# An eight-stage transformer kernel: the edges between the attentions in halves, and the last edge before the experts inside the expert steps

## The reference

```python
f0 = causal softmax attention with rotary positions, 16 heads of 8
f1 = feed-forward 128 -> 512 -> 128, SiLU, integer weights with scales, half of it added to its normed input
f2 = attention with its own norm, weights exp(s) * sigmoid(s - mu), normalised
f3 = gated feed-forward 128 -> 384 -> 128
f4 = linear attention (elu + 1), then a GELU feed-forward 128 -> 512 -> 128
f5 = 16 experts of 176, 4 chosen per token in 2 of 4 groups, and a shared expert
f6 = linear attention (elu + 1)
f7 = 8 experts of 512, 2 chosen per token
```

## Time and profile before

| | before |
|---|---|
| median of 3 runs | 1600.1 us (1598.7 to 1605.24) |
| the profiled execution | 1603.26 us |
| its span | 1601.5 us |
| TensorE busy in the span | 1281.2 us (80%) |
| VectorE | 1090.1 us (68%) |
| ScalarE | 1135.8 us (71%) |
| GpSimd | 279.3 us (17%) |
| mean granted TensorE clock | 0.884 |

### The profile page before, as it was taken

How to read it: one execution, slowest core, us unless ns; L and a number is a source line. 1 busy time by engine, 2 the same in 40 slices (tenths; PEclk the granted TensorE clock), 3 DMA queues, 4 the chain that set the end, 5 groups by cost and what they waited for, 6 DMA issues and landing times.

```text
span 1601.5 us, 22150 instructions
## 1 busy us (share of the span) xinstructions
PE 1281.2 (80%) x8028; PEld 650.2 (41%) x8028; DVE 1090.1 (68%) x2035; ACT 1135.8 (71%) x1607; POOL 279.3 (17%) x379
## 2 busy tenths in 40 slices
PE   5498888977687767777787778687999997888996
PEld 2233333345111111111111125466777775666775
DVE  6877877154266456656766575757988788766898
ACT  3166776755799999999999954454555655977985
POOL 4500003042000000001100013654011034813000
PEclk9589999888578877888788889997999998999998
DMA  5601120000601101001010030002332334010111
GB/s 183 154 22 23 23 42 3 2 1 12 185 1 20 20 0 20 18 18 20 1 20 1 1 139 1 1 1 60 114 88 90 106 94 159 14 34 29 46 47 53
DMA packets 40765, 74.65 MB, mean 47 GB/s; under 512 B 6096, under 2 KB 10448, under 8 KB 39888
## 3 DMA queue, kind: packets, MB, share of 16 engines
q1 hardware_dynamic: 39792, 71.67, 15.9%
q10 hardware_dynamic: 864, 1.57, 0.3%
HBM read 59.26 MB, written 13.96 MB: 46 GB/s over the span
## 4 chain that ended last, share of the span: by engine, by line
PE 38%; ACT 25%; DVE 20%; issue 13%; POOL 2%; DMA 1%; SPq 0%; DVEq 0%; ACTq 0%; POOLq 0%
ACT SHARED L1072 15%; PE PS L992 5%; PE PS L823 4%; PE PS L979 4%; DVE NM L732 3%; PE PS L645 3%; DVE KS L2031 2%; PE PS L712 2%; PE PS L787 2%; DVE SHARED L1082 2%; PE PS L1876 2%; PE PS L1256 2%; PE PS L1878 2%; PE PS L1877 2%; ACT ROUNDED L1965 1%
## 5 line engine op out<-in xcount | busy, mean ns | idle before, releaser
L1072 ACT ACTIVATE SHARED<-PS 128x1536 f32<-128x1536 f32 (+1 forms) x352 | 466.6, 1432 | 31.6 <-PE PS L979 30.2
L979 PE MATMUL PS<-QS,KS 51*128 51x512 bf16 (+1 forms) x1024 | 242.8, 463 | 129.4 <-ACT SHARED L1072 124.0
L1082 DVE TENSOR_TENSOR SHARED<-SHARED 128x1536 f32<-128x1536 f32 (+1 forms) x176 | 286.5, 1702 | 86.2 <-ACT SHARED L1072 86.2
L803 ACT ACTIVATE SHARED<-PS 128x512 f32<-128x512 f32 (+3 forms) x384 | 164.4, 493 | 100.8 <-PE PS L791 91.6
L979 PEld LDWEIGHTS PS<-QS,KS 51*128 51x128 bf16 (+1 forms) x1024 | 41.3, 99 | 378.1 <-ACT SHARED L1072 352.0
L992 PE MATMUL PS<-SHARED,Vg 128*16 128x512 f32 x1024 | 157.7, 693 | 1.8 <-DVE SHARED L1082 1.7
L732 DVE TENSOR_REDUCE NM<-PS 128x2 f32<-128x1024 f32 (+3 forms) x128 | 128.9, 1021 | 28.0 <-PE PS L718 19.9
L1876 PE MATMUL PS<-ROUNDED 128*128 128x512 f32 x328 | 137.1, 418 | 5.2 <-ACT KS L1977 4.5
L1878 PE MATMUL PS<-ROUNDED 128*128 128x512 f32 x328 | 131.1, 400 | 0.0
L1877 PE MATMUL PS<-ROUNDED 128*128 128x512 f32 x328 | 131.0, 400 | 0.0
L1965 ACT ACTIVATE ROUNDED<-KS 128x512 fp32r<-128x512 f32 x100 | 63.1, 631 | 91.5 <-DVE KS L2031 91.3
(11 more groups left out here) (267 smaller groups left out, 2273.9 us busy)
## 6 DMA issues: line engine op xcount, KB each, us to landing
SHARED<-wx SPq DMA_DIRECT2D x64, 256.0 KB, 3.2
qx<-SHARED SPq DMA_DIRECT2D x24, 256.0 KB, 4.0
SHARED<-in_moe SPq DMA_DIRECT2D x3, 1600.0 KB, 10.9
kx<-SHARED SPq DMA_DIRECT2D x18, 256.0 KB, 3.9
SHARED<-wx SPq DMA_DIRECT2D x16, 224.0 KB, 3.0
SHARED<-qx SPq DMA_DIRECT2D x16, 192.0 KB, 4.8
SHARED<-kx SPq DMA_DIRECT2D x16, 192.0 KB, 4.8
QS<-qx SPq DMA_DIRECT2D x16, 192.0 KB, 4.6
```

The lines of the kernel that those rows point to most:

```text
L803: act.activation(PB[t % 3][:, h, q0:CH], bank(RING0[n % 3], q0), ACT.Exp, scale=SCORE_SCALE)\
L979: ins = pe.matmul(bank((v % 2) * GRP + f - a), KS[g % 2][r, h // 2, kt * P:kt * P + P], QS[g % 2][r, h // 2, qh * CH:(qh + 1) * CH], start ...
L1072: act.activation(dst, PS[:, (v % 2) * GRP * CH:((v % 2) * GRP + b - a) * CH], ACT.Exp if second == qh else ACT.Sigmoid, scale=SCORE_SCALE)\
L1082: dve.tensor_tensor(ex_tile(j), ex_tile(j), GR[w % RING][:, 0:(b - a) * CH], ALU.mult)\
```

## The change

Between the attentions the two batches run half a stage apart. Batch 0's output projection, its edge 1 and its transposes stand in steps of groups 6 and 7 of the causal attention, with banks 1 and 3; two chunks of it are applied by POOL. f1 and f2's projections follow in an order written out by hand for each engine. Edge 5 of batch 1, its logits and scores move into the expert steps of chunk 0, batch 0's routing starts after its own scores, and batch 1's routing, the turn of its weights and their way to DRAM move to later steps.

```diff
+        QKB = (3, 1)
...
+        def pe_beside_attend0(pe, slots, g, s):
+            if (g, s) == (6, 9):
+                pe.wait_ge(A[0, "a_red"], slots.n)
+                pe_turn_out(pe, 0, 0, 1)
+            if (g, s) == (6, 10):
+                pe_turn_out(pe, 0, 1, 3)
+            if (g, s) == (7, 0):
+                pe_out_y(pe, 0, 0, "o0", None, 1)
+            if (g, s) == (7, 1):
+                pe_out_y(pe, 0, 1, "o0", None, 3)
+            if (g, s) == (7, 8):
+                pe_turn_x(pe, edges[1], 0)
+            if (g, s) == (7, 9):
+                pe_turn_x(pe, edges[1], 1)
+
+        def dve_beside_attend0(dve, own, g, s):
+            e = edges[1]
+            if g == 6 and s in (10, 11):
+                c = s - 10
+                dve.wait_ge(A[0, "aT"], c + 1)
+                dve.tensor_copy(chunk(hT, c), bank(2 * c + 1)).then_inc(A[0, "aTs"], 1)
+            if g == 7 and s in (1, 2):
+                dve_y(dve, own, e, s - 1)
+            if g == 7 and s in (3, 5):
+                dve_x(dve, own, e, s // 5)
+            if (g, s) == (7, 7):
+                dve_dequant0(dve)
+            if g == 7 and s in (9, 10):
+                c = s - 9
+                dve.wait_ge(xt_ready, e.n_x(c))
+                dve.tensor_scalar(chunk(hT, c), bank(e.t_at[c]), e.scale, e.bias, ALU.mult, ALU.add).then_inc(h_ready, 1)
+            if (g, s) == (7, 11):
+                dve_keep(dve, own, e, 0)
+                dve_keep(dve, own, e, 1)
...
+                    if (c, r) == (1, SHARED5 + 6):
                         sp_weights_out5(sp, 1)
...
+        def pe_first_between(pe):
+
+            e1, e2 = edges[1], edges[2]
+            pe.wait_ge(A[1, "f_w"], 1)
+            pe.wait_ge(h_ready, e1.n_x(1))
+            pe_ffn_up(pe, 1, e1, FW1, 0)
+            pe.wait_ge(A[0, "a_red"], NG * (NMAX + 1 + QH))
+            pe_turn_out(pe, 0, 2, 0)
+            pe_turn_out(pe, 0, 3, 2)
+            pe_ffn_up(pe, 1, e1, FW1, 1)
+            pe_out_y(pe, 0, 2, "o0", None, 6)
+            pe_out_y(pe, 0, 3, "o0", None, 7)
+            pe.wait_ge(cbase, NBASE + 1)
+            pe_ffn_down(pe, 1, FW2, HID0, RW["fc2b"], 0)
+            pe_ffn_down(pe, 1, FW2, HID0, RW["fc2b"], 1)
+            pe_turn_x(pe, e1, 2)
+            pe_turn_x(pe, e1, 3)
+            pe_ffn_up(pe, 1, e1, FW1, 2)
+            pe_ffn_up(pe, 1, e1, FW1, 3)
+            pe_ffn_down(pe, 1, FW2, HID0, RW["fc2b"], 2)
+            pe_turn_x(pe, e2, 0)
+            pe_ffn_down(pe, 1, FW2, HID0, RW["fc2b"], 3)
+            pe_turn_x(pe, e2, 1)
+            pe_qkv1(pe, 0)
+            pe_qkv1(pe, 1)
+            pe_turn_x(pe, e2, 2)
+            pe_turn_x(pe, e2, 3)
+            pe_qkv1(pe, 2)
+            pe_qkv1(pe, 3)
...
             pe_ffn_down(pe, 4, L2B, HID4, RW["fc2b2"], 2)
+            pe_turn_x(pe, edges[5], 0)
+            pe_turn_x(pe, edges[5], 1)
             pe_ffn_down(pe, 4, L2B, HID4, RW["fc2b2"], 3)
+            pe_logits(pe, 0)
+            pe_logits(pe, 1)
...
+            ffn(0)
+            act_attention_end(act, 0, (0, 2))
+            ffn(1)
+            act_apply(act, e1, 2)
+            act_apply(act, e1, 3)
+            act_turned(act, e1, 2)
+            act_turned(act, e1, 3)
+            ffn(2)
+            act_apply(act, e2, 0)
+            ffn(3)
+            act_apply(act, e2, 1)
+            act_turned(act, e2, 0)
+            act_turned(act, e2, 1)
+            act_qkv1(act, 0)
+            act_apply(act, e2, 2)
+            act_qkv1(act, 1)
+            act_apply(act, e2, 3)
+            act_turned(act, e2, 2)
+            act_turned(act, e2, 3)
+            act_qkv1(act, 2)
+            act_qkv1(act, 3)
...
             ffn(2)
+            act_apply(act, edges[5], 0)
             ffn(3)
...
-            if c == 0 and r == 20:
+            if c == 0 and r == 5:
+                pe.wait_ge(A[5, "cwTs"], 1)
+                pe_turn_x(pe, edges[5], 2)
+            if c == 0 and r == 6:
+                pe_turn_x(pe, edges[5], 3)
+            if c == 0 and r == 9:
+                pe.wait_ge(h_ready, edges[5].n_x(3))
+                pe_logits(pe, 2)
+            if c == 0 and r == 10:
+                pe_logits(pe, 3)
+            if c == 1 and r == 1:
                 pe_turn_weights5(pe, 1)
...
-                 1: Edge(1, 0, y_ready, eps2=1, keep=True, scale=col("g0"), bias=col("b0")),
-                 2: Edge(2, 1, y_ready, add=0.5, eps2=2, scale=col("g1"), bias=col("bb1")),
+                 1: Edge(1, 0, y_ready, y_at=(1, 3, 6, 7), t_at=(1, 3, 0, 2), pool_apply=(0, 1), eps2=1, keep=True, scale=col("g0"), bias=col("b0")),
+                 2: Edge(2, 1, y_ready, t_at=(0, 2, 0, 2), add=0.5, eps2=2, scale=col("g1"), bias=col("bb1")),
...
+        def dve_first_between(dve, own):
...
+            dve_y(dve, own, e1, 2)
+            dve_y(dve, own, e1, 3)
+            dve_x(dve, own, e1, 2)
+            dve_x(dve, own, e1, 3)
+            dve_y(dve, own, e2, 0)
+            dve_y(dve, own, e2, 1)
+            dve_x(dve, own, e2, 0)
+            dve_x(dve, own, e2, 1)
+            dve_keep(dve, own, e1, 2)
+            dve_keep(dve, own, e1, 3)
+            dve_y(dve, own, e2, 2)
+            dve_y(dve, own, e2, 3)
+            dve_x(dve, own, e2, 2)
+            dve_qkv1(dve, 0)
+            dve_x(dve, own, e2, 3)
+            dve_qkv1(dve, 1)
+            dve_qkv1(dve, 2)
+            dve_qkv1(dve, 3)
...
             dve_x(dve, own, e5, 1)
+            late(dve, 2)
             dve_y(dve, own, e5, 2)
+            dve_route5_a(dve, own, 0)
             dve_y(dve, own, e5, 3)
-            dve_x(dve, own, e5, 2)
-            dve_x(dve, own, e5, 3)
+            dve_route5_b(dve, own, 0)
+            dve_route5_c(dve, own, 0)
+            dve_route5_d(dve, own, 0)
...
+        def pool_first_between(pw):
...
+            for first in (0, 2):
+                pool_y(pw, e1, first)
+                pool_y(pw, e1, first + 1)
+                pool_x(pw, e1, first)
+                pool_x(pw, e1, first + 1)
+                pool_keep(pw, first)
+                pool_keep(pw, first + 1)
+            for first in (0, 2):
+                pool_y(pw, e2, first)
+                pool_y(pw, e2, first + 1)
+                pool_x(pw, e2, first)
+                pool_x(pw, e2, first + 1)
...
             pool_y(pw, e5, 3)
-            pool_x(pw, e5, 2)
-            pool_x(pw, e5, 3)
             pool_rest_of_h(pool, 5, 0)
             pool.wait_ge(A[5, "cw"], 1)
+            pool_x(pw, e5, 2)
+            pool_x(pw, e5, 3)
             splits(4)
...
-            pe.wait_ge(A[5, "sc"], B)
+            pe.wait_ge(A[5, "sc"], 1)
             pe_moe5(pe)
```

134 lines of the change are left out of this document (57 added, 77 removed).

## The result

The changed kernel took 1577.4 us (median of 4 runs, 1575.3 to 1580.2) against 1599.4 us (4 runs, 1597.1 to 1605.2) for the kernel before: a ratio of 0.9864 with a 95% interval of 0.9834 to 0.9895, so 22 us faster. A second comparison of the same pair, in another session, gave 1583.8 against 1595.2 us, ratio 0.9916 (0.9886 to 0.9945), 13 us by the ratio. The mean of the two ratios is 0.989, or 17.6 us; the forecast was 17.8 and the predicted time 1582.

The account below looks back on a forecast made before the run. Between the attentions it saw a latency chain over four chunks (edge, transpose, projection, split) with no engine full. Terms +2.0 - 22.4 + 2.6 = -17.8 us took the median from 1600.1 to 1582 us, range 1572 to 1592.

Parts of the forecast that it names:

- The attention's end: Causal attention's tail: six blocks added to TensorE's queue cost +2.0 us, bounds 0 and 3.6 (7 at the lower clock).
- Rival (5): Causal attention: the added blocks drop TensorE's clock for all 16 last steps, +22 us, net 1604; chance 0.03.
- Between the attentions: Feed-forward and second attention's projections: the new order brings the first gated activation to 397.3 from 419.7, -22.4 us.
- a tie with 0 to 2 us: Second attention's start: group 0's loads land at 396.0, when TensorE is ready too; costs 0, up to 2 us.
- Rival (4): Between the attentions: stacking DMAs or POOL roots end last, last two projections 3 us later each, 1588; chance 0.11.
- Rival (1): Projection stage between the attentions: full clock throughout, 5 us less, 1577; chance 0.13.
- Into the expert steps: Start of the expert steps: the first weighted step comes at 1099.3, not 1105.28, -6.0 us.
- Given back: Expert steps: splits and h subtractions +4.3, transposes and logits +1.5, scores +2.0, weights' turn +0.8, together 8.6 us.
- The transposes and logits: Expert steps 5 to 10: transposes, copies and logits of chunks 2 and 3 cost VectorE +1.5 us.
- The turn of the weights at (1,1): Expert step (1,1): batch 1's turn, moved where there is no weighting and TensorE is full, costs +0.8 us.
- Rival (2): Expert steps: POOL's splits and h subtractions are lost to VectorE one for one, 13.6 us not 6.5, 1589; chance 0.14.
- Rival (3): Expert steps: all 8.6 us of the give-back is hidden, 1573; chance 0.12.

## Why the prediction was right, point by point

**The attention's end: +2.0, measured +1.7.** 40.40 us became 42.12 from the 13th half group to the last. Later profiles tell it apart from the clock: where one interval in it is 8.84 us and not 11.54, it is 36.84 without the blocks and 38.48 with them, +1.6. VectorE's copies and statistics cost nothing there, as costed. Rival (5), a clock drop over the whole tail, did not occur in any profile; the 2.7 us between 8.84 and 11.54 occur with and without the change, at a granted clock of 1.00 and 0.65. Nor did the first sign of being wrong: TensorE does not wait for XN in group 7 (its transposes at 311.45 and 313.49 have no idle time before them).

**Between the attentions: -22.4, measured -20.8.** The order's gaps came out as laid by hand: up(0) right behind the transposes, waits at edge 1's chunks 2 and 3 (0.46 and 1.68 us, forecast 2.5 for the first), an apply ahead of up(3), 2.07 and 5.56 us for the second half (forecast 2.4 and 5.9). The terms that missed are three. Chunk 3's projection ran at the full level, 2 us shorter than costed; from the first way up to the last projection it took 65.5 us where 66.7 were laid out. The way from the last projection (386.7) to the table's end (394.48) is 7.8 us, not 6.1, because projections at full clock come faster than the split in three parts: ScalarE stands 1.24 us for VectorE's residue of chunk 2. And the load of group 0 ends 1.3 us later than that; the prediction had called it a tie with 0 to 2 us. The transfer was costed right (18.8 us from the first write to the first gated matmul, forecast 18.5); it began late, since the transposes behind down(3) ended 41.5 us behind the attention's last divided output, where 39.5 were laid out. In the prediction's words that was "what is late next", and "wrong if group 0's load releases the gated attention": it does, by 1.3 us. Rival (4) was thus true in kind and a quarter of its size. Rival (1) was half true, for one of two late projections.

**Into the expert steps: -6.0, measured -6.6** in the first pair of profiles and -6.3 over all. The path came out as forecast. Put on the old axis (24.45 us later, by edge 5's first `dve_x`), TensorE's first expert step came at 1086.5 (forecast 1086.5), the routing weights were done at 1089.9 (1090.0), and the first weighted step came at 1098.65 (1099.3). TensorE stood 7.10 us for the rest of h, which waits for chunk 3's statistics.

**Given back: 8.6, measured 8.1** (by the means of all profiles 7.6: 60.8 us where the old order has 53.1). The first seven weighted steps, with the splits and the subtractions of h, take 6.2 us more than seven of 1.99, and the old order's first step took 2.0 more than 1.99: that is +4.2, forecast +4.3. The scores cost 1.96, forecast 2.0. The transposes and logits were to cost 1.5 by their own length (the transposes lie in the seven steps above); the step at the logits took 3.96 us and not 1.99, so the size is near and the reason is another, the clock. Without the drop (2.24 and 2.21 us in the two profiles that have none) the term is a quarter of a us. The turn of the weights at (1,1) was to cost 0.8 and cost nothing: from chunk 1's first product to chunk 2's it is 61.60 to 61.64 us in all fourteen profiles, with the turn there or not. Rival (2), one for one, falls: three splits out of the steps gave back 3.3 us there, and one for one is 3 x 2.3 = 6.9. Both sides stretch: beside each other a split takes 1.25 + 1.89 us in place of 0.72 + 1.54, and a step 3.1 in place of 1.99, so about 1.1 us are VectorE's loss and 0.9 GpSimd's. The rule that the prediction weighed (the Trainium skill, SBUF — State Buffer, Who interferes with whom: the two exclude each other for the whole instruction when VectorE has two SBUF inputs) agrees in kind, and its exception does too: the product with one input in PSUM keeps its 0.68 us. An exclusion for the whole length of every instruction is not what the trace shows, though: two products of 0.69 and a split of 2.26 are 3.64 us together as recorded, and they pass in a step of 3.1. Of the loss VectorE bears about half. Rival (3), all of it hidden, falls too.

**The sum.** -17.8 forecast; -19.0 in the profiles without the stretch of unchanged code ahead of it, or -17.6 in the stages that have a term; 22 and 13 us by the two timed comparisons. That -17.6 is so near -17.8 is partly luck: between the attentions 1.6 us less was won, and 0.3, 0.6 and 0.5 us came back in the three other terms. The signs named beforehand came with it, once the 4.9 us that this execution was ahead are added: the first gated activation at 400.7 (near 399), the first weighted step at 1079.1 (near 1079), and chunk 0 of the experts 8.1 us longer (8). One did not: chunk 3's pair of projection passes took 1.12 us and not 1.7 (chunk 2's 1.84).

## What to carry to other kernels

Work whose latency is a chain of edges (statistics, root, apply, transpose) gains most by being put where another batch's stage keeps the engines fed: 12.8 us net here, against 6.3 for the order of the chain itself (one profile each, good to about 2 us). Moving work into a full stage must be costed by what each engine issues there, and also by who is starved by it: a few moves of GpSimd's and VectorE's pieces into their own idle time were worth 6.6 us, where the whole move at the experts by itself won nothing. When executions scatter by 0.5%, compare the length of the touched stage between two events of the trace; the times alone would have shown none of the single edits.

## What was not expected of the hardware

- Identical code in the causal attention took 10.79 or 12.11 us for a half group, and the 15th 8.84 or 11.54, from one execution to the next. The granted clock was 1.00 in the short ones, 0.86 in those of 12.11 and 0.65 in that of 11.54. They can make up to 9.3 us in one execution (five of 1.3 and one of 2.7), where 23 runs of one kernel lie 13 us apart; but of the 4.5 us between the two profiles of the changed kernel they are 1.3, so that they are most of the scatter is not shown.
- A TensorE that was starved by VectorE (0.95 us of work in 4 us) came back at a granted clock of 0.72 over 6 us, and then held VectorE up by 2.03 us. With 2.37 us of work in 4 the clock stayed at 1.00:

```profile
1104.67:1108.67 4.00, 2.37 (x10) 1.57 (x9) 3.74 (x6) 3.64 (x8) 1.27 (x1) 1.00 0.26 92
1108.67:1114.67 6.00, 6.00 (x34) 5.25 (x35) 5.73 (x9) 3.41 (x6) 1.58 (x1) 1.00 0.35 112
```

  These windows are of the kernel with the part at the experts alone, around the same logits. In the second profile of the changed kernel it was 2.27 us in 4 before and 0.72 after. What decides between the two is left open.
- Twelve writes of 256 KB took 11.9 us from their first issue to the first load's, and neither a second issuing queue nor half-sized writes brought the loads nearer: with the first the DMA engines were the limit, with the second SyncE's 24 issues of 0.64 us.
